# A fused attention and mixture-of-experts kernel: shared-expert tiles placed among the last row blocks, the last out-projection behind them, the row loads put ahead of the last expert weights, and the known experts' weights made the stationary operand

## The reference

```python
ctx = ctx.transpose(0, 2, 1, 3).reshape(N, t, H * DV)
s = ctx @ Wo + bo                                 # the out-projection
_, idx = jax.lax.top_k(scores + expert_bias, 4)   # 4 of 32 experts a token
# an expert: silu(clip(x @ wg.T, -7, 7)) * clip(x @ wu.T, -7, 7) @ wd.T, inner width 128
f = sum over the 4 experts of prob * expert(x)  +  shared_expert(x)
x = x + s * silu(f)
```

## Time and profile before

| | us |
|---|---|
| three timed runs, median (lowest, highest) | 889.47 (888.18, 890.79) |
| the profiled execution, its own time | 884.85 |
| its span in the profile | 883.1 |
| PE busy | 798.7 (90%) |
| VectorE busy | 621.6 (70%) |
| ScalarE busy | 447.9 (51%) |
| GpSimd busy | 426.8 (48%) |

### The profile page before, as it was taken

One profiled execution on the slowest core, in us unless ns is written; L12 is line 12 of the kernel. 1 busy time (PEld: TensorE's weight loads), 2 busy tenths in 40 slices (PEclk: granted clock), 3 DMA queues, 4 the chain that ended last, 5 costly groups with the idle time before them and its releaser, 6 DMA issues.

```text
span 883.1 us, 13675 instructions
## 1 busy us (share of the span) xinstructions
PE 798.7 (90%) x4707; PEld 632.4 (72%) x4707; DVE 621.6 (70%) x1115; ACT 447.9 (51%) x795; POOL 426.8 (48%) x474
## 2 busy tenths in 40 slices
PE   2999999988888866998899899999999999999996
PEld 2866666664223345777889788989999998887874
DVE  8377767458898855888895996767776655555556
ACT  3322231168666723476654656655666653555541
POOL 2466736334655533554532456676773310655550
PEclk9999999997787796999999999999999999999999
DMA  5121195000000004000000001110110477654307
GB/s 176 36 72 36 37 280 134 1 0 1 1 1 1 1 1 140 14 19 12 19 7 19 7 20 42 44 48 25 49 49 14 169 165 283 200 145 114 89 4 236
DMA packets 50114, 59.79 MB, mean 68 GB/s; under 512 B 13559, under 2 KB 41084, under 8 KB 50048
## 3 DMA queue, kind: packets, MB, share of 16 engines
q1 hardware_dynamic: 45488, 50.49, 19.1%
q0 software_dynamic: 4560, 8.44, 2.7%
HBM read 41.11 MB, written 21.86 MB: 71 GB/s over the span
## 4 chain that ended last, share of the span: by engine, by line
PE 71%; DVE 17%; issue 4%; ACT 4%; POOL 3%; DMA 0%; SPq 0%; DVEq 0%; ACTq 0%; POOLq 0%
PE ps L693 11%; PE ps L452 11%; PE ps L454 11%; PE ps L453 10%; PE ps L778 7%; PE ps L596 6%; PE ps L802 3%; DVE A L1245 3%; PE ps L533 2%; DVE swap L1309 2%; DVE cap L1319 2%; PE ps L516 2%; PE ps L491 2%; PE ps L759 2%; DVE qk_tok L1245 1%
## 5 line engine op out<-in xcount | busy, mean ns | idle before, releaser
L693 PE MATMUL ps<-V,P 128*128 128x129 f32 x1152 | 152.8, 279 | 0.0
L993 ACT ACTIVATE cap<-cap 128x1024 f32<-128x1024 f32 (+7 forms) x128 | 87.1, 680 | 123.6 <-DVE cap L1319 117.2
L693 PEld LDWEIGHTS ps<-V,P 128*128 128x128 f32 x1152 | 145.4, 194 | 2.7
L1319 DVE SCALAR_TENSOR_TENSOR cap<-dist,ps 128x1024 f32<-128x1024 f32 (+7 forms) x128 | 95.1, 749 | 25.6 <-PE ps L454 20.7
L1528 POOL TENSOR_SCALAR_AFFINE_SELECT P<-P 128x128 f32<-128x128 f32 x128 | 38.6, 302 | 149.5 <-ACT P L998 149.2
L1653 POOL DMA_INDIRECT y_scratch<-y_sb,aux_s x63 | 62.0, 984 | 64.5 <-issue 35.2
L998 ACT ACTIVATE P<-cap 128x1024 f32<-128x1024 f32 (+7 forms) x128 | 87.7, 685 | 4.1
L452 PE MATMUL ps<-q_hi,k_hi 128*128 128x512 f32 x192 | 72.2, 376 | 6.5 <-DVE cap L1319 6.2
L1245 DVE TENSOR_TENSOR A<-A 128x1024 f32<-128x1024 f32 (+4 forms) x60 | 63.0, 1104 | 9.0 <-ACT A L942 9.0
L778 PE MATMUL ps<-ew,xT 128*128 128x256 f32 (+1 forms) x252 | 67.2, 389 | 2.1 <-issue 1.2
L889 ACT ACTIVATE e_g<-ps 128x512 f32<-128x512 f32 x32 | 19.1, 597 | 96.7 <-PE ps L454 96.7
(11 more groups left out here) (265 smaller groups left out, 2022.1 us busy)
## 6 DMA issues: line engine op xcount, KB each, us to landing
xg_scratch<-blank SPq DMA_DIRECT2D x1, 8127.0 KB, 32.6
xa<-xg_scratch SPq DMA_DIRECT2D x63, 128.0 KB
ew<-in_experts SPq DMA_DIRECT2D x3, 1920.0 KB, 7.5
ew<-in_experts SPq DMA_DIRECT2D x2, 2688.0 KB, 9.7
y<-y_scratch SPq DMA_DIRECT2D x8, 512.0 KB, 5.8
pk<-in_packed SPq DMA_DIRECT2D x8, 384.0 KB, 3.0
pks<-in_scales SPq DMA_DIRECT2D x8, 384.0 KB, 3.9
wqk<-in_wqk SPq DMA_DIRECT2D x20, 128.0 KB
```

The lines of the kernel that those rows point to most:

```text
L693: last = pe.matmul(ps[:, 4 + r % 2, o:o + D1 + 1], P1[:, h % 2, a:a + P], V1[:, j, h // REP, :], start=(j == 0), stop=(j == t))
L993: act.activation(cap[:, n % 2, 0:w], cap[:, n % 2, 0:w], ACT.Tanh, scale=1.0 / (CAP * float(D1) ** 0.5))\
L1319: dve.scalar_tensor_tensor(out=cap[:, n % 2, 0:w], in0=dist[:, 0:w], scalar=slope, in1=psf[:, 1024 * (n % 2):1024 * (n % 2) + w], op0=ALU. ...
```

## The change

- `LINE` lays out the 71 places of the expert pipeline: blocks 0 to 54, then alternately a shared tile and a block (shared 0, block 55, ..., shared 7, block 62). Each stage works on a place p; `ROWS_AT[b]` is the place of block b.
- The last pair's 8 out-projection tiles leave `STEPS1` and stand behind the whole pipeline, in PSUM banks 0 and 1; `add_out` for them stands behind the pipeline on DVE. `down1(0)` now waits for the pair before alone.
- For known blocks the weights are stationary and the turned rows move (8 passes of 128 columns); the result comes out already turned, `inner` writes it to `hT1` directly, and `turn_inner` and `copy_inner` are left out for them.
- On the SP queue experts' group 4 is issued behind the rows of block 10, group 5 behind the rows of block 14.
- `yp` has 3 buffers, and DVE's order in the final sum is add_pairs(0), add_pairs(1), then add_pairs(t), final(t - 2).

```diff
...
 NSTEP = NBLK + NT
+LINE = ([("rows", b) for b in range(NBLK - NT)]
+        + [item for t in range(NT) for item in (("shared", t), ("rows", NBLK - NT + t))])
+ROWS_AT = [LINE.index(("rows", b)) for b in range(NBLK)]
 EGROUPS = [(0, 5), (5, 9), (9, 14), (14, 19), (19, 26), (26, 33)]
...
         hs = sb("hs", [P, NT, P])
-        yp = sb("yp", [P, 2, 2, D])
+        yp = sb("yp", [P, 3, 2, D])
         moe_pad = sb("moe_pad", [P, 32])
...
             sp.wait_ge(c_ps, 3 * H1)
-            for g in range(4, len(EGROUPS)):
-                load_experts(g)
             for b in range(NT, NBLK):
+                if b - NT in (3, 7):
+                    load_experts(4 if b - NT == 3 else 5)
                 sp.wait_ge(xg_ps, b - NT + 1)
...
                     pe.wait_ge(wo_ready, m + 1)
-                o = side_slot()
+                if m < H1 // PAIR - 1:
+                    o = side_slot()
+                else:
+                    pe.wait_ge(xg_copied, NBLK)
+                    if t >= 2:
+                        pe.wait_ge(s_added, NT * m + t - 1)
+                    o = ps[:, t % 2, :]
                 tk = slice(t * P, (t + 1) * P)
...
-            def gate_up1(b):
-                if b >= 2:
-                    pe.wait_ge(clip_ready, b - 1)
-                for g, (first, end) in enumerate(EGROUPS):
-                    if b == first:
-                        pe.wait_ge(in_ew[g], 16)
-                o = ps[:, 2 + b % 2, 0:2 * P].rearrange("p (m n) -> p m n", m=2)
-                if b < NBLK:
+            def gate_up1(p):
+                kind, b = LINE[p]
+                if p >= 2:
+                    pe.wait_ge(clip_ready, p - 1)
+                o = ps[:, 2 + p % 2, 0:2 * P].rearrange("p (m n) -> p m n", m=2)
+                if kind == "rows":
+                    for g, (first, end) in enumerate(EGROUPS):
+                        if b == first:
+                            pe.wait_ge(in_ew[g], 16)
                     pe.wait_ge(xg_copied, b + 1)
...
                     w = weights(b)
-                    for c in range(NC):
+                    for m, c in ((0, 0), (0, 1), (1, 0), (1, 1)) if b < NE else ():
+                        last = pe.matmul(o[:, m, :], w[:, m, c * P:(c + 1) * P], xT1[:, b % 3, c, :], start=(c == 0),
+                                         stop=(c == NC - 1))
+                    for c in range(NC) if b >= NE else ():
                         last = pe.matmul(o, xT1[:, b % 3, c, :], w[:, 0:2, c * P:(c + 1) * P], start=(c == 0),
...
                     pe.wait_ge(ws_ready, 1)
-                    tk = slice((b - NBLK) * P, (b - NBLK + 1) * P)
+                    tk = slice(b * P, (b + 1) * P)
                     for c in range(NC):
...
-            def turn_inner(b):
-                pe.wait_ge(h1_ready, b + 1)
+            def turn_inner(p):
+                pe.wait_ge(h1_ready, p + 1)
+                if p == NE:
+                    pe.wait_ge(c_ready, 3 * H1)
+                if p >= NE + 2:
+                    pe.wait_ge(hT_copied, p - NE - 1)
+                pe.transpose(ps[:, 4 + p % 2, 0:P], h1[:, p % 2, :], ident[:]).then_inc(hT_ps, 1)
+            def down1(b):
+                p = ROWS_AT[b]
+                if b < NE:
+                    pe.wait_ge(h1_ready, p + 1)
+                else:
+                    pe.wait_ge(hT_copied, p - NE + 1)
                 if b == 0:
-                    pe.wait_ge(c_ready, 3 * H1)
-                if b >= 2:
-                    pe.wait_ge(hT_copied, b - 1)
-                pe.transpose(ps[:, 4 + b % 2, 0:P], h1[:, b % 2, :], ident[:]).then_inc(hT_ps, 1)
-            def down1(b):
-                pe.wait_ge(hT_copied, b + 1)
-                if b == 0:
-                    pe.wait_ge(s_added, (H1 // PAIR) * NT)
+                    pe.wait_ge(s_added, (H1 // PAIR - 1) * NT)
+                    pe.wait_ge(cT_ready, 2 * H1)
                 if b >= 2:
...
             def moe(s):
-                if s < NBLK:
-                    turn_rows(s)
+                if s < NSTEP and LINE[s][0] == "rows":
+                    turn_rows(LINE[s][1])
                 if 0 <= s - 1 < NSTEP:
                     gate_up1(s - 1)
-                if 0 <= s - 2 < NSTEP:
+                if NE <= s - 2 < NSTEP:
                     turn_inner(s - 2)
-                if 0 <= s - 3 < NBLK:
-                    down1(s - 3)
+                if 0 <= s - 3 < NSTEP and LINE[s - 3][0] == "rows":
+                    down1(LINE[s - 3][1])
...
                 pe.wait_ge(pair_ready, t + 1)
-                pe.wait_ge(hT_copied, NBLK + t + 1)
+                pe.wait_ge(hT_copied, NSTEP - NE)
                 if t == 0:
...
                 for i in range(2):
-                    pe.matmul(o, ident[:], yp[:, t % 2, i, :], start=(i == 0), stop=False)
+                    pe.matmul(o, ident[:], yp[:, t % 3, i, :], start=(i == 0), stop=False)
                 pe.matmul(o, hs[:, t, :], expert(NE)[:, 2, :], start=False, stop=True).then_inc(fin_ps, 1)
...
-            for s in range(MOE_EARLY, NSTEP + 2):
+            for s in range(MOE_EARLY, NSTEP + 3):
                 moe(s)
+            for t in range(NT):
+                project_out1(H1 // PAIR - 1, t)
             for t in range(NT):
...
                     dve.wait_ge(s_added, NT * m)
-                dve.tensor_tensor(s_tok[:, t, :], ps[:, 6 + side_of["out", m, t] % 2, 0:D],
+                b = 6 + side_of["out", m, t] % 2 if m < H1 // PAIR - 1 else t % 2
+                dve.tensor_tensor(s_tok[:, t, :], ps[:, b, 0:D],
                                   bo[:] if m == 0 else s_tok[:, t, :], ALU.add).then_inc(s_added, 1)
...
-            def clip(b):
-                dve.wait_ge(gu1_ps, b + 1)
-                if b == 0:
+            def clip(p):
+                dve.wait_ge(gu1_ps, p + 1)
+                if p == 0:
                     dve.wait_ge(s1_exp, NT * H1)
-                if b >= 2:
-                    dve.wait_ge(silu_ready, b - 1)
-                dve.tensor_scalar(gu[:, b % 2, :], ps[:, 2 + b % 2, 0:2 * P], ALPHA, -ALPHA, ALU.min, ALU.max)\
+                if p >= 2:
+                    dve.wait_ge(silu_ready, p - 1)
+                dve.tensor_scalar(gu[:, p % 2, :], ps[:, 2 + p % 2, 0:2 * P], ALPHA, -ALPHA, ALU.min, ALU.max)\
                     .then_inc(clip_ready, 1)
-            def inner(b):
-                dve.wait_ge(silu_ready, b + 1)
-                if b >= 2:
-                    dve.wait_ge(hT_ps, b - 1)
-                dve.tensor_tensor(h1[:, b % 2, :], sg[:, b % 2, :], gu[:, b % 2, P:2 * P], ALU.mult).then_inc(h1_ready, 1)
-            def copy_inner(b):
-                dve.wait_ge(hT_ps, b + 1)
-                if 2 <= b < NBLK:
+            def inner(p):
+                kind, b = LINE[p]
+                known = kind == "rows" and b < NE
+                dve.wait_ge(silu_ready, p + 1)
+                if known and b >= 2:
                     dve.wait_ge(dn1_ps, b - 1)
-                dst = hT1[:, b % 2, :] if b < NBLK else hs[:, b - NBLK, :]
-                dve.tensor_copy(dst, ps[:, 4 + b % 2, 0:P]).then_inc(hT_copied, 1)
+                if p >= NE + 2:
+                    dve.wait_ge(hT_ps, p - NE - 1)
+                dst = hT1[:, b % 2, :] if known else h1[:, p % 2, :]
+                dve.tensor_tensor(dst, sg[:, p % 2, :], gu[:, p % 2, P:2 * P], ALU.mult).then_inc(h1_ready, 1)
+            def copy_inner(p):
+                kind, b = LINE[p]
+                dve.wait_ge(hT_ps, p - NE + 1)
+                if kind == "rows":
+                    dve.wait_ge(dn1_ps, b - 1)
+                dst = hT1[:, b % 2, :] if kind == "rows" else hs[:, b, :]
+                dve.tensor_copy(dst, ps[:, 4 + p % 2, 0:P]).then_inc(hT_copied, 1)
...
                     clip(s - 1)
-                if s >= 2:
+                if NE <= s - 2 < NSTEP:
                     copy_inner(s - 2)
...
+            for t in range(NT):
+                add_out(H1 // PAIR - 1, t)
             def add_pairs(t):
                 dve.wait_ge(in_y4[t % YLOADS], 16 * (t // YLOADS + 1))
-                if t >= 2:
-                    dve.wait_ge(fin_ps, t - 1)
-                dve.tensor_tensor(yp[:, t % 2], y4[:, t, 0:2], y4[:, t, 2:4], ALU.add).then_inc(pair_ready, 1)
-            for t in range(NT + 1):
+                if t >= 3:
+                    dve.wait_ge(fin_ps, t - 2)
+                dve.tensor_tensor(yp[:, t % 3], y4[:, t, 0:2], y4[:, t, 2:4], ALU.add).then_inc(pair_ready, 1)
+            for t in range(NT + 2):
                 if t < NT:
                     add_pairs(t)
-                if t >= 1:
-                    r = t - 1
+                if t >= 2:
+                    r = t - 2
                     dve.wait_ge(fth_ready, r + 1)
...
     steps += [("moe", s) for s in range(MOE_EARLY)]
-    steps += [("out", H1 // PAIR - 1, t) for t in range(NT)]
     return steps
```

(52 more changed lines are left out.)

## The result

The changed kernel takes 891.13 us (median of 20 runs, 886.84 to 895.00), the kernel before, run beside it, 887.92 us (20 runs, 883.15 to 892.34). The ratio is 1.0047, with a 95% interval of 1.0029 to 1.0065: slower by half a percent, where 0.3% faster was forecast, and outside the range. The profiled execution took 891.13 us with a span of 889.4. The forecast for it was 882.0, so 9.1 are to be found.

A forecast was written before the change was run, and what follows sets the result against it. PE was taken to bound the experts' pipeline, loads and VectorE the final sum. Terms of -0.64 up to the last down product and -2.2 behind it gave -2.84, from 889.47 to 886.6 us; range 883.2 to 890.8.

The forecast's parts named there:

- Step 1: Before pipeline step 3: the last out-projection leaves (-5.99), with a transpose and the wait for its input (-0.35).
- Step 2: Known blocks: no transpose, 8 passes of 128 columns; a step takes 1.54, 0.09 less, -2.6 over 29 steps.
- Step 4: Drain: the last block's chain, gate and up to down product, takes 1.9 with 0.65 of covering work, +1.25.
- step 7: Final sum: out-projection hidden before it; three buffers space tiles 1.40 apart, -2.2 (0 to -2.6).
- Step 5: Blocks beyond 32: run-time weight overhead of 0.20 a block stays, shared tiles barely covered; +0.2 (-1.6 to +0.8).
- Step 6: SP queue and DMA: rows behind weight groups 4 and 5 come late for block 15, +0.9 (0 to 3).
- Rival A: Known blocks' gate and up: weight loads bind at 128 columns, a step 0.54 longer, 904.9 us; chance 0.04.
- Steps 3 to 5: From pipeline step 32: step 3 counts six more shared tiles and five more transposes, +5.95; Step 4 and Step 5 follow.
- Rival B: Expert pipeline: results starve behind weight loads, a stall of 5.2 replaces the 0.9, 891.0 us; chance 0.14.
- rival D: Final sum: loads of y bound it, so the gain of 2.2 is not there, 888.8 us; chance 0.17.
- Rival C: All gains, no costs: rows never late, mixed steps hide the overhead of 8 blocks; -5.5, 883.9 us; chance 0.18.

The follow-up runs named there:

- swapped: The kernel with both repairs, with the block ahead of the shared tile in each pair and the last down product ahead of the last tile's transpose: 878.17 us, ratio 0.9909.
- read behind: The changed kernel with the register read of the next block's weight place moved behind the gate and up products: 886.64 us, ratio 0.9994.
- group 5 later: The changed kernel with weight group 5 issued behind the rows of block 19 instead of block 14: 888.51 us, ratio 1.0016.
- both repairs: The changed kernel with the register read behind the gate and up products and weight group 5 behind block 19's rows: 880.75 us, ratio 0.9932.
- moving weights: The swapped kernel with known experts' weights moving again (4 passes of 256 columns) and their inner activations transposed: 882.44 us, ratio 0.9946.
- The kernel with two buffers: Two yp buffers and one add ahead, against the both repairs kernel with shared tiles last and out-projection tiles between them: 879.22 us, ratio 0.9923 against 0.9862.
- shared tiles last and both repairs: The kernel with both repairs, with all eight shared tiles behind the 63 blocks instead of between the last ones: 879.66 us, ratio 0.9925.

## Why the prediction was wrong, step by step

It named the right places, and steps 1, 2 and 4 came out as worked, step 7 in its number but not in its parts; steps 5 and 6, both in the experts' pipeline, were undersized. Forecast against trace, from the same row, the last down product is 8.7 late and the end 0.9 better; with 1.3 of drift ahead of the change that is the 9.1.

- **Step 1, out-projection moved: right.** -6.28 measured, -6.34 forecast.
- **Step 2, stationary weights: right.** A step of 1.553 for 1.54; -2.4 over 29 steps for -2.6, and -2.6 up to block 32 between the two swapped kernels. Rival A is dead: 8 passes take 0.89 to 0.90 beside loads of 0.19 each, so the rule of the Trainium skill ("TensorE: Matmul & The Clock Gate", "The mechanism") that wants another row group for the overlap does not hold for these rows. The same section of the Trainium skill also lets a load into the background weight buffer go ahead of running products, which would fit; no run here tells whether that is what happens.
- **Steps 3 to 5 together: +12.1 for +7.4. Step 5 failed.** It said that the overhead of run-time weights "stays" and that a shared tile's chain is "barely enough" cover, and put +0.2 on the mixed stretch. The pair of 3.47 where 2.9 were expected makes 8 x 0.57 = 4.6 of it. The error has two halves. The first: the 0.20 a block was not looked into. It was one register read, queued behind the wait for the copied rows, so that in the pair the read began only once the copy was there: 0.91 from copy to product with it, 0.24 without. The second, which follows from the order of the program and was not tested by itself: in a full step, down product and turning of the next rows stand between a block's copy and its products, and cover most of that. In the pair neither does: the place behind a block is a shared tile, which has no rows to turn, and so is the place three ahead of it, which has no down product. So a latency that cost 0.19 in a full step cost 0.46 in a thinned one. Its price was taken from a place with cover and carried to one without. Moving the read took 0.46 off each pair, 3.7 of the 4.6; 0.9 are left, 0.11 a pair, and the tile's own chain is the likely place, since PE waits 0.37 for it once the read is gone.
- **Step 4, drain: right.** 2.1 for 1.9.
- **Step 6, the stall at block 15: right in place and kind, +4.6 for +0.9**, and over its upper end of 3. The rows came at 763.8, not 760.6: row 15 was issued at 749.05 behind group 5, 2688 KB of weights, and needed 14.7 us, while the DMA engines were full (their share of busy time was 1.02 to 1.07 from 746 to 764). Of the 3.2, 1.3 is the drift ahead of the change. The rest is traffic that the sum did not have. From 742 to 764 the SP queue moved 6.97 MB and the results 1.18. Less the 5.51 MB of the two groups (the step's 5.38 is 2688 KB twice in another unit than its rows, 0.3 us too little) this leaves 1.46 MB of rows, where the step had 0.66: the other 0.8 MB, rows issued just before group 4 or behind row 15, are 2.0 us at 396 GB/s (an estimate; how it splits between the two isn't known). Block 15's step is 2.8 longer by the wait. Another 1.7 was no term at all in the sum: the two steps behind the wait, at the lower clock. Rival B, results starving, did not come; the wait is for `xa`, not for `y_sb`, and from 749 to 764 a result landed in a median of 5.6 us.
- **Step 7, the end: -3.1 for -2.2, beyond its own lower end of -2.6, and in part by luck.** From down product to first load 4.22 for 4.23. But the sum itself became 1.4 shorter, not 2.2 (15.74 against 17.13), since its first tile ran at the lower clock. It began 1.7 earlier behind the down product (8.91 against 10.59), which the step had left out: the first tile came 3.9 behind the load, not 5.6, because before, VectorE had still been copying shared tiles. And the loads do bind: VectorE waits 2.5 us for them in the changed kernel, 0.4 before. In the other kernels with pairs it waits 3.8 to 7.6, and of the gain from down product to end 2.1 (swapped), 1.7 (read behind), 1.2 (group 5 later), 0.5 (both repairs) or nothing (moving weights, 1.6 longer than before) is left. So rival D is true in part where the sum starts 9 to 11 us behind the last down product. The kernel with two buffers confirms the buffer's 2.2 only for a sum that starts 13.9 behind it, where the loads are well ahead.
- **Rival C** ("gains, no costs", 883.9) was the closest in kind to the repaired kernel, 880.75: the overhead of run-time weights was indeed idle time that could be taken, but by moving the read and not by a shared tile laid over it.

The range failed with them: the upper ends of the unknown costs were +0.8 for step 5 and 3 for step 6, and the trace has some 4.9 (0.2 and the 4.7 that were missing) and 4.6. Slower had 0.13, since no rival joined the two. That the measured time lies only 0.3 outside the range owes something to luck: the end came out 0.9 better than forecast, and the 889.47 from which the forecast was carried over was the median of three runs, 1.6 above the 887.92 of all twenty.

## What to carry to other kernels

A latency read from a full pipeline is what is left of it behind its cover; before work is taken out of, or put between, such steps, find the instruction that makes it, and count it whole. A register read or any other set-up of the next step goes behind the products, not between a wait and them. Where PE is made to wait, price the wait and the steps behind it: here a wait of 2.6 us cost 4.5. A row load queued behind weights must be dated by the bytes ahead of it and a margin for the other loads that move beside it. And a change of many parts should be compared with its cheapest part alone: here one moved read gave as much as the whole repaired change.

## What the runs showed of the hardware that was not expected

TensorE's granted clock fell to its lower level (0.50) behind idle times of 2.6 us (two steps 1.75 longer in all), 6.2 us (two steps 2.0 longer), 3.87 us and, before the sum of the changed kernel, 2.12 us. But the length of the last idle time does not decide it alone. Before the same sum in the kernel with the read behind the products, PE idled 2.08 us and its clock stayed at 1.00. In front of the sum of the kernel that is the one before with only the read moved, it idled 0.67 and then 0.98 us, and the clock fell. The kernel before idled 0.90 and 0.98 us there and kept its clock. The first tile of the sum in the two kernels, the second nearly twice as long:

```profile
864.14 1.13 PE L843 MATMUL ps<-yp,ident 128*128 128x256 f32 x4 [2.08 <-DVE yp L1535]
```

```profile
857.04 2.07 PE L824 MATMUL ps<-yp,ident 128*128 128x256 f32 x4 [0.98 <-DVE yp L1504]
```

A register read of PE between a wait and a product costs 0.67 us there (0.91 less 0.24), as idle time of the weight loads without a releaser.

VectorE sometimes starts a clip over 1 us late although its input is there, and PE's step is then 0.7 to 1.6 longer. PE, then VectorE, in the kernel with shared tiles last and both repairs:

```profile
766.88 1.06 PE L782 MATMUL ps<-xT,ew 128*128 128x128 f32 x8
```

```profile
769.21 0.42 DVE L1485 TENSOR_SCALAR gu<-ps 128x256 f32<-128x256 f32 x1 [1.69 <-PE ps L782]
```

The products are done at 766.88 + 0.89 = 767.8, and their clip starts at 769.21. It happened at one to three places among the known blocks in eight of the eleven kernels with stationary weights, and in none of the three with moving weights. But three with stationary weights are free of it: the changed kernel, the one with both repairs and the one with swapped pairs. It is therefore not simply a price of stationary weights. With shared tiles last it stood at blocks 20 and 31 in two kernels and at other blocks in the other three. It took up to 3.2 us from a run, as much as the effects that some of the experiments looked for. Which of the queues, the fetching of VectorE's instructions or the order of semaphores causes it was not tried, and stays open.
